# Second cross-attention: the key bias of two heads of a quad on GpSimd through SBUF, of two on VectorE, none on TensorE; four score banks and two of shifted scores

## The reference

```
q = (layernorm(x) @ Wq.T + bq) * 8 ** -0.5
k = context @ Wk.T + bk
v = context @ Wv.T + bv
scores = einsum('bhld,bhsd->bhls', q, k) + attn_mask[None, None]   # attn_mask: 256 x 256, float32
scores = where(key_padding_mask[:, None, None, :], -inf, scores)
attn = einsum('bhls,bhsd->bhld', softmax(scores), v)
x = x + attn @ Wo.T + bo
```

## Time and profile before

| | |
|---|---|
| median of 3 runs | 608.61 us (608.24 to 612.67) |
| the profiled execution | 611.73 us |
| its span, first to last instruction | 610.0 us |
| TensorE busy | 526.7 us (86%) |
| VectorE busy | 452.4 us (74%) |
| ScalarE busy | 263.2 us (43%) |
| GpSimd busy | 134.5 us (22%) |
| mean granted clock of TensorE | 0.944 of full speed |
| chain that ended last, by engine | TensorE 66%, VectorE 23%, issue 5%, ScalarE 4%, GpSimd 2% |

### The profile page before, as it was taken

One profiled execution on the slowest core, in us unless ns is written; L12 is line 12 of the kernel. 1 busy time (PEld: TensorE's weight loads), 2 busy tenths in 40 slices (PEclk: granted clock), 3 DMA queues, 4 the chain that ended last, 5 costly groups with the idle time before them and its releaser, 6 DMA issues.

```text
span 610.0 us, 9155 instructions
## 1 busy us (share of the span) xinstructions
PE 526.7 (86%) x3260; PEld 298.6 (49%) x3268; DVE 452.4 (74%) x1175; ACT 263.2 (43%) x455; POOL 134.5 (22%) x101
## 2 busy tenths in 40 slices
PE   3997799999999999999999944655668999999886
PEld 1344666665666566566665500222224655555433
DVE  6599667676575366676456789999996778889786
ACT  5531256556433144243243346555521454444553
POOL 8443000000000000040000018899990100000100
PEclk9999799999998899999999985987788999999899
DMA  5000070000010000100000000000001000000001
GB/s 131 24 16 1 18 225 3 1 2 2 6 38 1 1 0 2 34 6 1 1 0 2 1 0 0 0 0 1 1 0 44 2 1 2 2 2 1 2 5 30
DMA packets 10768, 9.26 MB, mean 15 GB/s; under 512 B 2050, under 2 KB 9540, under 8 KB 10724
## 3 DMA queue, kind: packets, MB, share of 16 engines
q1 hardware_dynamic: 10724, 8.69, 5.0%
HBM read 6.98 MB, written 0.52 MB: 12 GB/s over the span
## 4 chain that ended last, share of the span: by engine, by line
PE 66%; DVE 23%; issue 5%; ACT 4%; POOL 2%; POOLq 0%; DVEq 0%; ACTq 0%
PE PS L1154 18%; PE PS L716 10%; PE PS L1180 9%; PE PS L779 5%; DVE PS L1713 5%; DVE VA L1726 5%; PE PS L764 3%; PE PS L755 3%; DVE PS L1719 2%; PE PS L692 2%; PE PS L736 2%; PE PS L455 1%; PE PS L287 1%; PE PS L433 1%; PE PS L789 1%
## 5 line engine op out<-in xcount | busy, mean ns | idle before, releaser
L1154 PE MATMUL PS<-XNT,KSA 128*128 128x512 f32 x256 | 121.5, 609 | 0.0
L941 ACT ACTIVATE E<-PS 128x512 f32<-128x512 f32 x128 | 71.2, 596 | 67.2 <-PE PS L764 41.7
L1168 DVE TENSOR_TENSOR E<-E,PS 128x512 f32<-128x512 f32 x64 | 43.9, 687 | 58.5 <-ACT E L1162 57.5
L1162 ACT ACTIVATE E<-PS 128x512 f32<-128x512 f32 x64 | 38.1, 597 | 108.4 <-PE PS L1154 108.2
L764 PE MATMUL PS<-QM,KP 32*128 32x256 f32 x512 | 81.3, 399 | 0.8 <-ACT E L941 0.8
L716 PE MATMUL PS<-KP,QP 32*128 32x256 f32 x512 | 78.6, 412 | 0.4 <-ACT QP L908 0.4
L1180 PEld LDWEIGHTS PS<-KSA,E 128*128 128x128 f32 x512 | 62.4, 192 | 16.8 <-issue 15.5
L1154 PEld LDWEIGHTS PS<-XNT,KSA 128*128 128x128 f32 x256 | 46.2, 195 | 42.8 <-issue 42.8
L1180 PE MATMUL PS<-KSA,E 128*128 128x128 f32 x512 | 62.4, 275 | 0.4 <-DVE XN L1389 0.4
L716 PEld LDWEIGHTS PS<-KP,QP 32*128 32x128 f32 x512 | 51.5, 191 | 20.8 <-issue 10.3
L292 PE MATMUL PS<-KSA,select 128*128 128x512 bf16 x62 | 24.9, 489 | 41.3 <-ACT KSA L1614 31.2
(11 more groups left out here) (280 smaller groups left out, 859.6 us busy)
## 6 DMA issues: line engine op xcount, KB each, us to landing
KSA<-in_w SPq DMA_DIRECT2D x2, 1024.0 KB, 6.9
X<-in_x SPq DMA_DIRECT2D x2, 256.0 KB, 3.3
SCR<-in_ctxT SPq DMA_DIRECT2D x1, 512.0 KB, 5.6
KP<-OT SPq DMA_DIRECT2D x16, 32.0 KB
SCR<-in_fside SPq DMA_DIRECT2D x1, 512.0 KB, 4.6
KP<-QM SPq DMA_DIRECT2D x16, 32.0 KB
out_x<-X SPq DMA_DIRECT2D x8, 64.0 KB, 1.5
wx<-in_w_x SPq DMA_DIRECT2D x1, 384.0 KB, 6.6
```

What stands on the lines that cost most here:

```text
L941: act.activation(slot(m, j), weight_bank(m, j), ACT.Exp).then_inc(sig("exps"), 1)
L1154: ins = pe.matmul(bank(2 * (g % 3) + o), w[:, e, c * P:(c + 1) * P], XNT[:, tokens_of(p)], start=True, stop=True)
L1162: act.activation(E6[:, 4 + g % 2, :], bank(2 * (g % 3)), ACT.Silu).then_inc(sig("silu"), 1)
L1168: dve.tensor_tensor(E6[:, g % 4, :], E6[:, 4 + g % 2, :], bank(2 * (g % 3) + 1), ALU.mult)\
```

## The change

In the second cross-attention (L = 1) TensorE's three bias matmuls for heads 0 and 2 are gone, with the three-part mask `BIASK` and the GpSimd work that made it. Heads 2 and 3 have their key bias added by VectorE in the bank, as heads 1 and 3 had. For heads 0 and 1 ScalarE copies the shifted scores to SBUF (`loosen`), GpSimd adds the bias there, and ScalarE takes the exponential from SBUF into the slot (`late_exps`, behind the steps for heads 2 and 3). The copy frees the bank and counts in `exps`. The weighing waits for `late_exps` too. Scores get four banks (0 to 3) and wait for the maximum of the item four before; shifted scores have two (4 and 5) and wait for the copy or exponential of the item two before. GpSimd's 32 additions stand in its list ahead of the additions and powers for the feed-forward. The first cross-attention is as before.

The diff, without the declaration of `BIASK`:

```diff
@@ -632,11 +630,13 @@
         FIRST_ITEMS = 2 * HG
-        def score_bank(n, i):
+        def score_bank(L, n, i):
             item = HG * n + i
-            return bank(item % HG if item < FIRST_ITEMS else item % 3)
-
-        def score_bank_free(item):
+            return bank(item % HG if L == 1 or item < FIRST_ITEMS else item % 3)
+
+        def score_bank_free(L, item):
+            if L == 1:
+                return item - HG + 1
             if item < HG:
                 return 0
@@ -644,8 +644,8 @@
                 return item - HG + 1
             return (7, 5, 6)[item - FIRST_ITEMS] if item < FIRST_ITEMS + 3 else item - 2
-        def weight_bank(m, j):
-            return bank(3 + (HG * m + j) % 3)
+        def weight_bank(L, m, j):
+            return bank(4 + j % 2 if L == 1 else 3 + (HG * m + j) % 3)
         def slot(m, j):
             return E8[:, (HG * m + j) % 8, :]
@@ -659,7 +659,17 @@
         def vector_bias(L, j):
-            return L == 1 and j % 2 == 1
+            return L == 1 and j >= LOOSE_HEADS
+
+        def pool_bias(L, j):
+
+            return L == 1 and j < LOOSE_HEADS
+
+        LOOSE_HEADS = 2
+
+        def loose(m, j):
+            k = LOOSE_HEADS * (m % 2) + j
+            return VAf[:, 2 * T + k * HALF:2 * T + (k + 1) * HALF]
         def turn_bank(L, b, q):
             return bank(7) if b < B - 1 else bank((4, 3)[L] + q)
@@ -710,10 +720,10 @@
                 elif i == 0 and (g == 0 or n == NG - 1):
                     pe.wait_ge(sig("queries"), L * B + b + 1)
                 if item >= HG:
-                    pe.wait_ge(sig("maxed"), I0 + score_bank_free(item))
+                    pe.wait_ge(sig("maxed"), I0 + score_bank_free(L, item))
                 for q in range(QT):
                     t = b * S + q * P
-                    ins = pe.matmul(score_bank(n, i)[:, q * S:(q + 1) * S], QP[rows(i), g, t:t + P],
+                    ins = pe.matmul(score_bank(L, n, i)[:, q * S:(q + 1) * S], QP[rows(i), g, t:t + P],
                                     KP[rows(i), g, b * S:(b + 1) * S], start=True, stop=True, skip_group_check=True)
                 ins.then_inc(sig("scores"), 1)
@@ -736,39 +746,39 @@
                     ins = pe.transpose(bank(7)[:, q * P:(q + 1) * P], MXT[:, n % 2, q, :], ident[:, :])
                 ins.then_inc(sig("max_turned"), 1)
-            def parts_of_bias(j):
-                return L == 1 and not vector_bias(L, j)
-
             def shifted_bank(m, j):
                 item = HG * m + j
-                if item == 0:
-                    pe.wait_ge(sig("maxed"), I0 + FIRST_ITEMS)
-                if item == 2:
-                    pe.wait_ge(sig("queries"), L * B + 3)
-                if item >= 3:
-                    pe.wait_ge(sig("exps"), I0 + item - 2)
-                return weight_bank(m, j)
-
-            def bias_rows(m, j):
-                o = shifted_bank(m, j).rearrange("p (k n) -> p k n", k=QT)
-                for c in range(3):
-                    pe.matmul(o, identb[:, :], BIASK[:, :, c, :], start=(c == 0), stop=False, skip_group_check=True)
+                if L == 0:
+                    if item == 0:
+                        pe.wait_ge(sig("maxed"), I0 + FIRST_ITEMS)
+                    if item == 2:
+                        pe.wait_ge(sig("queries"), L * B + 3)
+                    if item >= 3:
+                        pe.wait_ge(sig("exps"), I0 + item - 2)
+                else:
+                    if item < 2:
+                        pe.wait_ge(sig("queries"), L * B + 2 + item)
+                    else:
+                        pe.wait_ge(sig("exps"), I0 + item - 1)
+                return weight_bank(L, m, j)
             def shifted_scores(m, j):
                 b, g = where(m)
                 i = head_of(j)
                 pe.wait_ge(sig("shifted"), N0 + m + 1)
-                o = weight_bank(m, j) if parts_of_bias(j) else shifted_bank(m, j)
+                o = shifted_bank(m, j)
                 for kt in range(QT):
                     t = b * S + kt * P
                     ins = pe.matmul(o[:, kt * S:(kt + 1) * S], KP[rows(i), g, t:t + P],
-                                    QM[rows(i), g, b * S:(b + 1) * S], start=not parts_of_bias(j), stop=True,
+                                    QM[rows(i), g, b * S:(b + 1) * S], start=True, stop=True,
                                     skip_group_check=True)
                 ins.then_inc(sig("shifted_scores"), 1)
             def weigh(m):
                 b, g = where(m)
                 pe.wait_ge(sig("exps"), I0 + HG * (m + 1))
+                if L == 1:
+                    pe.wait_ge(sig("late_exps"), LOOSE_HEADS * (m + 1))
                 if m == 0:
                     pe.wait_ge(sig("queries"), L * B + 4)
                 if m % 2 == 0 and m:
@@ -844,9 +854,6 @@
             def pair(k, first):
                 m = k - LAG
-                for j in (first, first + 1):
-                    if 0 <= m < QUADS and parts_of_bias(j):
-                        bias_rows(m, j)
                 for j in (first, first + 1):
                     if k < QUADS:
                         scores(k, j)
@@ -935,10 +942,21 @@
             def exps(m, j):
                 act.wait_ge(sig("shifted_scores"), I0 + HG * m + j + 1)
                 if vector_bias(L, j):
-                    act.wait_ge(sig("biased"), 2 * m + j // 2 + 1)
+                    act.wait_ge(sig("biased"), (HG - LOOSE_HEADS) * m + j - LOOSE_HEADS + 1)
                 if m >= 2:
                     act.wait_ge(sig("weighed"), N0 + m - 1)
-                act.activation(slot(m, j), weight_bank(m, j), ACT.Exp).then_inc(sig("exps"), 1)
+                act.activation(slot(m, j), weight_bank(L, m, j), ACT.Exp).then_inc(sig("exps"), 1)
+
+            def loosen(m, j):
+
+                act.wait_ge(sig("shifted_scores"), I0 + HG * m + j + 1)
+                act.activation(loose(m, j), weight_bank(L, m, j), ACT.Copy).then_inc(sig("exps"), 1)
+
+            def late_exps(m, j):
+                act.wait_ge(sig("loose_biased"), LOOSE_HEADS * m + j + 1)
+                if m >= 2:
+                    act.wait_ge(sig("weighed"), N0 + m - 1)
+                act.activation(slot(m, j), loose(m, j), ACT.Exp).then_inc(sig("late_exps"), 1)
             def out_take(z):
                 b, x = divmod(z, 2)
@@ -955,7 +973,12 @@
                 b, s = out_step(k)
                 for j in range(HG):
                     if k - LAG < QUADS:
-                        exps(k - LAG, j)
+                        if pool_bias(L, j):
+                            loosen(k - LAG, j)
+                        else:
+                            exps(k - LAG, j)
+                        if L == 1 and j >= 2:
+                            late_exps(k - LAG, j - 2)
                     if j == 1 and k == FEED_FRONT + 1:
                         if L == 0:
                             moe_root(act, ch, 0)
@@ -986,7 +1009,7 @@
             def maximum(n, i):
                 dve.wait_ge(sig("scores"), I0 + HG * n + i + 1)
                 c = 32 * i + MAX_ROW
-                o = score_bank(n, i).rearrange("p (q n) -> p q n", q=QT)
+                o = score_bank(L, n, i).rearrange("p (q n) -> p q n", q=QT)
                 if L == 0:
                     ins = dve.tensor_reduce(MXT[:, n % 2, :, c], o, AX, ALU.max, negate=True)
                 else:
@@ -1009,7 +1032,7 @@
                 dve.wait_ge(sig("shifted_scores"), I0 + HG * m + j + 1)
                 if m == 0:
                     dve.wait_ge(sig("bias_in"), 16 * 4)
-                o = weight_bank(m, j)
+                o = weight_bank(L, m, j)
                 dve.tensor_tensor(o, o, BIASF, ALU.add).then_inc(sig("biased"), 1)
             def divide(b, q):
@@ -2018,6 +2041,10 @@
             pool.wait_ge(sig("xn"), 2 * 6)
             pool.tensor_tensor(X[:, :, :], X[:, :, :], bobc.unsqueeze(1).to_broadcast([P, NT, D]), ALU.add)\
                 .then_inc(sig("x_biased"), 1)
+            for m in range(QUADS):
+                for j in range(LOOSE_HEADS):
+                    pool.wait_ge(sig("exps"), ITEMS + HG * m + j + 1)
+                    pool.tensor_tensor(loose(m, j), loose(m, j), BIASF, ALU.add).then_inc(sig("loose_biased"), 1)
             add_bias(0)
             power(0, tiles_of(1), "feed_variance", 2)
             add_bias(1)
@@ -2112,13 +2139,7 @@
             x_ready(pool, 2)
             pool.wait_ge(sig("fside_in"), 16)
             pool.wait_ge(sig("w_quantised"), 2)
-            pool.tensor_scalar(BIASQ, FRAW[:, 0:QT, :], 1.0, 0.0, ALU.mult, ALU.add)
-            ch.link(pool.tensor_scalar(BIASK[:, :, 0, :], FRAW[:, QT:, :], 1.0, 0.0, ALU.mult, ALU.add))
-            rest = KXR[:, 0:QT * S].rearrange("p (w n) -> p w n", w=QT)
-            ch.link(pool.tensor_tensor(rest, FRAW[:, QT:, :], BIASK[:, :, 0, :], ALU.subtract))
-            ch.link(pool.tensor_scalar(BIASK[:, :, 1, :], rest, 1.0, 0.0, ALU.mult, ALU.add))
```

(5 more changed lines are left out.)

## The result

The change makes the kernel slower: median 628.22 us (627.4 to 628.94, 4 runs) against 608.42 (607.83 to 612.67, 4 runs), a ratio of 1.033 with a 95% interval of 1.0299 to 1.0361. The forecast was 618.5 with a range of 612 to 623. The direction was right, the size half of what came. The profiled execution took 627.67 us, its span is 625.2. In the ratios of this document executions over 1.5% above the fastest of the same kernel are left out (one of banks33, one of no_last_add); the medians are of all.

What follows compares the result with a forecast made beforehand. TensorE was taken as the bound, then a loop through two shifted-score banks: twelve rounds +7.9, first rounds +0.2, last rounds +1.7 and 0.1, together +9.9 on the 608.61 us median, giving 618.5, range 612 to 623.

Steps and rivals of the forecast that it cites:

- TensorE is the bound today: Twelve rounds of the second cross-attention, kernel before: TensorE busy 64.22 of 64.73 us, the bias matmuls on the path.
- The ceiling of the gain is 7.6 us: In the twelve rounds VectorE's own work, 57.16 of 64.73 us, limits the gain to 7.6 us.
- A round takes 6.05 us: Predicted length of each of the twelve rounds after the change, against 5.39 before; together +7.9 us.
- the loop: Head 3's addition, exponential, head 1's shifted scores, turn, head 2's scores, VectorE again: 6.05 us a round; chance 0.68.
- VectorE idles some 1.7 of it: Claim that VectorE stands idle for some 1.7 us of each 6.05 us round.
- The fourth score bank buys nothing in this loop: Claim that the scores VectorE waits for stand behind head 1, not behind a bank; no gain.
- First rounds: Up to quad 3's shift: head 1 of quad 0 waits for ScalarE's four copies; +0.2 us, between -1.5 and +1.5.
- The collision of VectorE and GpSimd: Feed-forward centring and rounding in rounds 15 and 16 against GpSimd's additions; up to 2.5 us more, outside the sum.
- Last rounds: After the last shift: later output step, rounding and last additions +1.7 us, late exponential +0.1; bounds 0 to 3.
- rival 3: The loop binds and TensorE's clock falls too: +9 us if low for a third of the rounds, 627; chance 0.07.
- short stop of TensorE: Stop of TensorE in each round, named as why its clock might fall; 2.2 us more a round at the low clock.

Runs made afterwards that it cites:

- banks33: Changed kernel with the three score and three shifted-score banks of before, and their waits; bias work as in the change: 611.79 us, ratio 1.0047.
- no_last_add: Changed kernel; GpSimd's last-quad bias additions cut to one column, its first addition to x held until the feed-forward's first rounding: 623.51 us, ratio 1.0219.
- mix_PVTV: Kernel before, its banks kept, with GpSimd instead of TensorE adding head 0's bias up to quad 13: 603.34 us, ratio 0.9904.
- fill2: Changed kernel plus two full-row TensorE matmuls a round whose result is overwritten: 630.09 us, ratio 1.0359.
- banks_only: Kernel before with only the change's four score and two shifted-score banks and their waits; bias matmuls stay: 640.62 us, ratio 1.0536.
- b33_tail: Changed kernel with the old three and three banks, VectorE's feed-forward scaling and rounding moved behind the last key bias additions: 609.28 us, ratio 1.0033.
- mix_PPPV: Changed kernel with three and three banks; up to quad 13 GpSimd adds heads 0 to 2, VectorE head 3; then VectorE all: 616.87 us, ratio 1.0143.
- turn_first: Changed kernel with the turn of the maxima put ahead of the shifted scores of heads 0 and 1 on TensorE: 646.24 us, ratio 1.0627.

## Why the prediction was wrong

- **"TensorE is the bound today."** Right. mix_PVTV takes half of the bias matmuls away and gains 3.6 us in the rounds, the expected 3 to 5 in the time.
- **"The ceiling of the gain is 7.6 us."** Not contradicted: the best of these kernels reached 3.6.
- **"A round takes 6.05 us."** Measured 6.05 to 6.07 in seven of the twelve rounds, 5.88 and 5.96 in two. The mechanism is right: each step is as added up, except that the item started 0.14 us after the exponential instead of 0.05, and the turn 1.03 after the item instead of 1.10. That these two cancel to 0.01 is luck. banks33 shows that the two banks close the loop. Twelve rounds cost 12 x 0.66 = +7.9 as forecast. "VectorE idles some 1.7 of it" was too much: 6.05 less 57.16 / 12 = 4.76 of work is 1.3, and the two waits measured are 0.82 and 0.63.
- **"The fourth score bank buys nothing in this loop."** Not contradicted: banks33, with three, is the faster one.
- **First rounds, +0.2 within -1.5 and 1.5.** +1.0 by fill2, at the high clock, and +0.9 by the changed kernel's own rows.
- **The collision of VectorE and GpSimd, "up to 2.5 us higher".** It came, at 2.0 us, and on the path. It had been left out of the sum for want of a row; the sentence drawn from the Trainium skill had it right. In banks33, where a third addition follows, it was 3.1.
- **Last rounds, +1.8 within 0 and 3.** The time from the last shift to the end of the last weighing rose by 6.3 us (from 8.5 to 14.8), and behind it 0.3 are gained. Of the +6.0 the clock is 2.8 (below), the collision 2.0, and 1.2 are left for the order.
- **The step that failed: "for rival 3 ... against it: TensorE would still be busy some nine tenths of a round, and the first stage with such staggered items ran at 1.00", chance 0.07.** The clock fell, and the cost of that had been put at nothing in the sum. TensorE's busy share was 97.9% in the twelve rounds of the changed kernel (73.82 of 75.41), so the busy share was no argument. The first stage was no like case: it goes through four items abreast in 4.05 us, this one needs 6.06 for the same. The "short stop of TensorE" that rival 3 named isn't enough as a reason either: banks_only stops for longer (busy 78.19 of 86.16 us), has its bias matmuls, and kept 1.00. What the low clock cost is read from rows at either level:

```profile
490.05 1.93 PE L789 MATMUL PS<-E,VX 128*32 128x256 f32 x16
...
516.25 1.07 PE L789 MATMUL PS<-E,VX 128*32 128x256 f32 x16
```

The weighing (L789, sixteen matmuls) takes 1.07 us at the high level (2.4 GHz) and 1.93 at the low one (1.2 GHz), 1.8 times the length, the sign that the prediction gave for rival 3. At the end the chain of waits has these pieces, in the kernel before (L779 weighing, L789 turn of the output) and in the changed one (L772 shifted scores, L789 weighing, L799 turn of the output), where the granted clock was 0.50 from 572 to 585:

```profile
561.79 1.00 PE PS L779 x16
562.79 0.60 PE PS L789 x4
...
569.29 1.07 PE PS L779 x16
```

```profile
570.82 2.07 PE PS L772 x7
572.90 1.87 PE PS L789 x16
574.76 1.06 PE PS L799 x4
...
584.34 1.51 PE PS L789 x16
```

In the twelve rounds the excess over 6.05 is 75.41 - 72.6 = 2.8 us; at the start, 1.1; at the end two weighings are 0.9 and 0.4 longer, shifted scores 1.0 (2.07 instead of 1.1) and a turn 0.5, together 2.8. That makes 6.7 us of the 18.8.

Rival 3 had +9 on top of 618.5, 627, and the kernel took 628.2. That it comes so near is in part luck. Its price of 2.2 us for a round at the low clock fits: some 11 of the 75.41 us were low, a seventh and not a third, and cost 2.8. But its +9 was meant for the twelve rounds alone; the rest of the clock's cost lay ahead of them and behind them, and the collision and the order made up the difference. The mechanism was on the list with its price, and its chance was far too low.

In sum: loop 7.9, first rounds 1.0, order at the end 1.2, collision 2.0, clock 6.7: 18.8.

What stays open: the clock's price was not measured by itself in the changed kernel. Filling holds the clock up but lengthens rounds, so the 6.7 us are worked out from rows and not from a difference of two times; the nearest to such a difference is the 1.4 us at the end of b33_tail. Why the clock falls isn't shown either. That banks33 (5.28 us a round, no bias matmuls) kept 1.00 in the twelve rounds of its trace, and mix_PPPV (5.81) did not, fits the reading of less full-width work in more time, and so does banks_only, but no run varies it alone.

## What to carry to other kernels

Before taking a bank from a pipeline, ask for each item what must happen before its bank comes free, and what stands behind the waiting item in its engine's order; such a loop can be added up beforehand from rows, here to 0.01 us in sum and 0.1 in its steps. A busy share doesn't tell whether TensorE keeps its clock: here, with full-width work gone and narrow items spread out, it fell at 98% busy. And when work moves to GpSimd, look for what VectorE does from SBUF to SBUF at that time; the whole change lost 3.3%, with the old banks the same bias work lost 0.5%, and with the old banks and only one of TensorE's two heads handed over, none in the last quads, 1.0% was gained.

## What the runs showed of the hardware that I had not expected

- TensorE's granted clock was 0.50 from 491 to 500 us in the changed kernel, with the engine busy 10.00 of 10.00 us; with four or two full-width matmuls added a round (three of them took 0.81 us) it was 1.00 in these rounds.
- Four VectorE instructions of 0.88 us together took 4.00 us beside three GpSimd additions of 1.25 us; VectorE's maxima, with an operand in PSUM, took 0.42 us with and without such additions.
- With the items issued in another order (turn_first), the scores of head 2 started 0.97 us after the shifted scores of the same rows (509.76 and 510.73), with no wait at a semaphore in the trace; in the order of before, the first matmuls of four items start within 0.04 us (514.71 to 514.75).
